# A decoder layer on one core: the first steps written out in another order, a fifth shared group ahead of the sorted experts, and routed rows added by TensorE

## The reference

```python
x = x + attn(layernorm(x))        # 16 heads of 8; att = softmax(q k^T / sqrt(8) * tril(k=-1)); out @ Wr + br
x = x + xattn(layernorm(x), ctx)  # q = x W + b; softmax(q ctx^T) ctx, with 1601 context rows a batch
x = x + ffn(layernorm(x))
# ffn: scores = softmax(x gate^T); the top 2 of 8 experts by scores + bias
#   y = sum over the 2 chosen of weight * (silu(x w1^T) * (x w3^T)) w2^T
#   z = the same MLP with the shared weights sw1, sw2, sw3, for every token
#   result y + z
```

## Time and profile before

| | |
|---|---|
| median of 3 runs | 725.09 us (723.1 to 729.39) |
| the profiled execution | 724.58 us |
| its span, first to last instruction | 722.5 us |
| around the span | 2.08 us |
| TensorE, ScalarE, GpSimd, VectorE busy | 87%, 66%, 64%, 59% of the span |
| mean granted TensorE clock | 0.966 of full speed |

### The profile page before, as it was taken

The page is one execution under the profiler, slowest core; times in us unless marked ns, Lnnn a source line. Parts: engine busy times, 40 slices in busy tenths (PEclk is TensorE's granted clock), DMA queues, the critical chain, the costliest instruction groups (busy, mean ns, idle before and its releaser), DMA issues.

```text
span 722.5 us, 17210 instructions
## 1 busy us (share of the span) xinstructions
PE 631.4 (87%) x5461; PEld 492.1 (68%) x5504; DVE 426.9 (59%) x1166; ACT 477.1 (66%) x1108; POOL 462.6 (64%) x780
## 2 busy tenths in 40 slices
PE   1546789998999999999999999999988679999994
PEld 0323456776767777677776777767877558888883
DVE  1335556686776877768767686775546523333337
ACT  3124558778787787877878778677777326666650
POOL 5034656578787787877877778667654606666660
PEclk9968989999999999999999999999999979999997
DMA  2444354633535235353353433513311223333129
GB/s 71 99 81 133 94 148 132 173 86 108 149 83 157 72 122 149 85 154 97 105 147 82 154 99 102 155 26 109 103 50 60 77 63 99 87 90 89 56 64 308
DMA packets 65110, 77.94 MB, mean 108 GB/s; under 512 B 9314, under 2 KB 50679, under 8 KB 64896
## 3 DMA queue, kind: packets, MB, share of 16 engines
q1 hardware_dynamic: 60672, 68.39, 34.5%
q0 software_dynamic: 4352, 8.47, 3.8%
HBM read 54.30 MB, written 22.64 MB: 106 GB/s over the span
## 4 chain that ended last, share of the span: by engine, by line
PE 37%; POOL 28%; issue 17%; DMA 6%; DVE 4%; SPq 4%; ACT 3%; POOLq 0%; another core or an unknown queue 0%; ACTq 0%; DVEq 0%
PE banks L322 7%; POOL prob L1893 6%; POOL sorted_rows L1918 5%; PE banks L344 4%; PE banks L1010 4%; POOL rstd L1804 3%; PE banks L972 3%; PE banks L752 3%; POOL info_lo L1882 3%; DMA k_stack<-parts 2%; PE banks L333 2%; PE banks L992 2%; POOL qk_r L1831 2%; DMA qst<-q_parts 2%; POOL parts L1833 2%
## 5 line engine op out<-in xcount | busy, mean ns | idle before, releaser
L1332 ACT ACTIVATE prob<-banks 128x512 f32<-128x512 f32 x192 | 114.7, 598 | 67.1 <-PE banks L755 66.5
L1893 POOL TENSOR_SCALAR_AFFINE_SELECT prob<-prob 128x256 f32<-128x256 f32 (+1 forms) x192 | 91.8, 500 | 69.2 <-ACT prob L1332 68.8
L752 PE MATMUL banks<-kst,qst 48*128 48x128 bf16 (+1 forms) x512 | 77.0, 252 | 43.3 <-DMA qst<-q_parts 16.3
L1520 DVE TENSOR_REDUCE mx<-banks 128x2 f32<-128x512 f32 x128 | 86.9, 680 | 33.8 <-PE banks L762 32.8
L1010 PE MATMUL banks<-info,xprobT 128*128 128x128 f32 (+1 forms) x832 | 103.9, 276 | 0.0
L1010 PEld LDWEIGHTS banks<-info,xprobT 128*128 128x128 f32 (+1 forms) x832 | 100.4, 192 | 1.4
L1516 DVE TENSOR_REDUCE mx<-banks 128x4 f32<-128x512 f32 x64 | 44.1, 689 | 73.9 <-remote 39.4
L752 PEld LDWEIGHTS banks<-kst,qst 48*128 48x128 bf16 x512 | 29.2, 95 | 81.2 <-DMA qst<-q_parts 25.2
L1918 POOL DMA_INDIRECT sorted_rows<-row,place x64 | 64.8, 1013 | 24.4 <-issue 18.3
L1551 DVE TENSOR_REDUCE xmax<-banks 128x1 f32<-128x896 f32 x64 | 63.0, 984 | 23.7 <-PE banks L972 18.5
L755 PE MATMUL banks<-qst,kst 51*128 51x128 bf16 (+1 forms) x512 | 75.7, 250 | 0.1
(11 more groups left out here) (193 smaller groups left out, 1591.7 us busy)
## 6 DMA issues: line engine op xcount, KB each, us to landing
infoT<-in_ctxT SPq DMA_DIRECT2D x16, 800.5 KB, 5.3
info<-in_ctx SPq DMA_DIRECT2D x16, 448.0 KB, 3.7
kst<-k_stack SPq DMA_DIRECT2D x32, 192.0 KB
info<-in_ctx SPq DMA_DIRECT2D x16, 320.0 KB
q_parts<-parts SPq DMA_DIRECT2D x32, 96.0 KB, 2.3
k_stack<-parts SPq DMA_DIRECT2D x32, 96.0 KB, 2.3
qst<-q_parts SPq DMA_DIRECT2D x32, 96.0 KB
infoT<-sorted_rows SPq DMA_DIRECT2D x36, 65.0 KB
```

The lines of the kernel that those rows point to most:

```text
L752: pe.matmul(alpha_bank[:, c * w:(c + 1) * w], lhsT=q[:, h, qs], rhs=k[:, h, keys], start=(c == 0), stop=False, skip_group_check=True)
L1332: act.activation(prob[n % 2][:, kind * 512:(kind + 1) * 512], ps[:, gamma_bank_of(b, v), :], ACT.Exp, scale=SCALE).then_inc(s["p_exp"], 1)
L1520: dve.tensor_reduce(mx[:, 1, h:h + 2, 0], bank.rearrange("p (c n) -> p c n", c=2), AX.X, ALU.max).then_inc(s["alpha_max"], 1)
L1893: pool.affine_select(out=w, in_=w, compare_op=ALU.is_gt, fill=0.0, base=0, pattern=[[0, 4 if kind == 2 else 2], [1, P]], channel_multiplie ...
```

## The change

It has four parts.

1. **Head.** The steps -3 to 2 are no longer run by `step(i)`, but written out for each engine in a function `begin()`; the loop starts at 3. The work is the same and the order is another one: both halves of batch 0's parts are written before either is loaded, batch 1 is projected ahead of batch 0's scores, and `x` and the first `infoT` are loaded at the very start. Since the DRAM buffers of the parts are now written sooner, `write_parts` waits until the last `load_stack` of that half has landed.
2. **Banks.** For batches 0 to 2 (`WIDE` = 3), odd units of alpha use bank 0 (6 for batch 0), and for batches 0 and 1 odd units of gamma use bank 1. These banks belong to the cross-attention's scores, which begin after that; its first one waits for alpha and gamma to be done.
3. **Finish.** `EARLY` becomes 5: a fifth shared group runs ahead of the sorted stage. The lists in `finish()` are reordered on every engine but SP.
4. **Tail.** Three shared groups are left. For these TensorE adds the routed rows itself, by multiplying them with the identity matrix into the bank that holds the shared result (`add_routed`, 2 f32 matmuls of 512 columns a group), and VectorE adds that bank to `xall` in one go (`add_late`). Loads and sums run in a mixed order of groups.

The core of the diff, without most of the lists:

```diff
@@ -41,6 +41,7 @@
+WIDE = 3
...
-EARLY = NGR // 2
+EARLY = 5
...
+        LATE_BANKS = (4, 7, 5)
+        SUM_ORDER = (0, 1, 5, 2, 6, 3, 7, 4)
+        BACK_ORDER = (0, 5, 1, 6, 2, 7, 3, 4)
...
-                after(pe, "shared_done", g - 1)
+                    pe.wait_ge(s["shared_done"], EARLY)
                 for t in range(GT):
                     for z in range(2):
-                        mm = pe.matmul(ps[:, Y_BANKS[g % 2], t * D:(t + 1) * D], lhsT=h[g % 2][z][:, t * P:(t + 1) * P],
-                                       rhs=w2_sb[:, E, z, :], start=(z == 0), stop=(z == 1))
+                        mm = pe.matmul(ps[:, LATE_BANKS[g - EARLY], t * D:(t + 1) * D], lhsT=h[g % 2][z][:, t * P:(t + 1) * P],
+                                       rhs=w2_sb[:, E, z, :], start=(t == 0 and z == 0), stop=False, skip_group_check=True)
                 mm.then_inc(s["y_ps"], 1)
+
+            def add_routed(g):
+
+                pe.wait_ge(s[f"back{g}"], 16 * TOPK)
+                for k in range(TOPK):
+                    mm = pe.matmul(ps[:, LATE_BANKS[g - EARLY], :], lhsT=ident, rhs=back[k][:, GT * g:GT * g + GT, :].rearrange("p t d -> p (t d)"),
+                                   start=False, stop=(k == TOPK - 1), skip_group_check=True)
+                mm.then_inc(s["late_ps"], 1)
...
-            def shared(g0, g1):
-                for g in range(g0, g1):
-                    for z in range(2):
-                        shared_up(g, z)
-                    if g > g0:
-                        shared_down(g - 1)
-                shared_down(g1 - 1)
+            def late_groups():
+
+                shared_up(5, 0)
+                shared_up(5, 1)
+                shared_up(6, 0)
+                shared_up(6, 1)
+                shared_down(5)
+                shared_up(7, 0)
+                shared_up(7, 1)
+                shared_down(6)
+                add_routed(5)
+                shared_down(7)
+                add_routed(6)
+                add_routed(7)
...
+            def add_late(g):
+
+                dve.wait_ge(s["late_ps"], g - EARLY + 1)
+                xg = xall[:, GT * g:GT * g + GT, :]
+                dve.tensor_tensor(xg, ps[:, LATE_BANKS[g - EARLY], :].rearrange("p (t d) -> p t d", t=GT), xg, ALU.add).then_inc(s["tokens_done"], 1)
+
             def add_back(g):
                 xg = xall[:, GT * g:GT * g + GT, :]
                 dve.wait_ge(s[f"back{g}"], 16 * TOPK)
                 dve.wait_ge(s["shared_done"], g + 1)
-                for k in range(TOPK):
-                    if k:
-                        dve.wait_ge(s["sum_done"], 2 * g + 1)
-                    dve.tensor_tensor(xg, back[k][:, GT * g:GT * g + GT, :], xg, ALU.add).then_inc(s["sum_done"], 1)
+                final(10 + g, dve.tensor_tensor(xg, back[0][:, GT * g:GT * g + GT, :], xg, ALU.add))
+                dve.tensor_tensor(xg, back[1][:, GT * g:GT * g + GT, :], xg, ALU.add).then_inc(s["tokens_done"], 1)
...
+                for g in SUM_ORDER:
+                    if g < EARLY:
+                        add_back(g)
+                    else:
+                        add_late(g)
...
-        STEPS = range(-3, B)
+        STEPS = range(3, B)
...
-            return G_BANK if b == 0 and u % 2 else A_BANK
+            if u % 2 and b < WIDE:
+                return G_BANK if b == 0 else 0
+            return A_BANK
 
         def gamma_bank_of(b, u):
 
+            if u % 2 and b < WIDE - 1:
+                return 1
             return A_BANK if b == B - 1 and u % 2 else G_BANK
 
...
                 if live(b):
                     sp.wait_ge(s["split_sub"], 2 * b + 2)
+                    after(sp, f"stack{a}_in", 64 * b)
...
+            def begin():
+
+                later_inputs(-1)
+                later_inputs(0)
+                load_infoT(0)
+                write_parts(0, 0)
+                write_parts(0, 1)
+                load_stack(0, 0)
+                load_stack(0, 1)
+                write_parts(1, 0)
+                write_parts(1, 1)
+                load_w13(0)
+                load_stack(1, 0)
+                write_maxima(0)
+                load_info(0, 0)
+                load_stack(1, 1)
+                load_w13(1)
+                later_inputs(2)
...
-            for g in range(NGR):
+            for g in BACK_ORDER:
...
-            for g in range(NGR):
-                sp.wait_ge(s["sum_done"], 2 * g + 2)
+            for n, g in enumerate(SUM_ORDER):
+                sp.wait_ge(s["tokens_done"], n + 1)
...
-                    after(pe, "alpha_max", 12 * b + u - (b == 0))
+                    after(pe, "alpha_max", 12 * b + u - (b < WIDE))
...
-                    after(pe, "p_exp", 12 * old + u - (old == B - 1))
+                    after(pe, "p_exp", 12 * old + u - (old < WIDE - 1 or old == B - 1))
...
+                    if k == 0:
+                        pe.wait_ge(s["alpha_max"], 12 * WIDE)
+                        pe.wait_ge(s["p_exp"], 12 * (WIDE - 1))
...
+            def begin():
+
+                norms_T(-1)
+                query_key(-1)
+                value_heads(0)
+                value_sums(0)
+                norms_T(0)
+                query_key(0)
+                scores(0, 0)
+                scores(0, 1)
+                scores(0, 2)
...
+                early_down(1)
+                early_up(3, 0)
                 norms_T(B + 3)
                 gate_logits(B + 3)
-                early_down(1)
-                early_up(3, 0)
                 early_down(2)
+                early_up(3, 1)
                 ranks(B + 3)
-                early_up(3, 1)
                 early_down(3)
-
+                early_up(4, 0)
+                early_up(4, 1)
+                early_down(4)
...
-                shared_lo(2)
                 deviation3(B - 2)
                 send_rows(B - 3)
+                row_inputs(B - 2)
                 cross_diff(B - 1)
+                shared_lo(2)
                 cross_den(B - 1)
                 cross_weight(B - 1)
-                row_inputs(B - 2)
-                deviation3(B - 1)
                 shared_lo(3)
                 send_rows(B - 2)
+                deviation3(B - 1)
+                shared_lo(4)
                 row_inputs(B - 1)
                 send_rows(B - 1)
-                shared_lo(4)
                 shared_lo(5)
-
+                shared_lo(6)
```

567 lines of the change are left out of this document (433 added, 134 removed).

## The result

In 11 runs of each on one chip, the changed kernel takes 718.99 us (714.86 to 723.03) and the kernel before 727.96 us (722.78 to 735.49). The ratio is 0.989, with a 95% interval of 0.986 to 0.993: about 8 us, or 1.1%, faster. The forecast was 12.6 us. The profiled execution takes 718.32 us with a span of 716.2 us, against 724.58 and 722.5 before: 6.3 us. The sign was right and the size too large, so each term must be held against the trace. In later batches of runs the kernel before took 728.6, 730.5, 754.4 and 761.6 us, and the other kernels moved with it, so each experiment is held against the kernel before of its own batch.

A forecast was written before the change was run, and what follows sets the result against it. TensorE, busy 87% of the span, was read as the main engine, with DMA bounding the tail. The sum was 724.58 - 10.4 (head) + 0.7 (finish) - 0.3 (fifth group) - 2.2 (tail) = 712.4 us profiled; forecast 712.5, range 706 to 719.

The forecast's parts named there:

- The head up to step 2: From the start to maxima_T of step 2: 97.7 to 87.3, a gain of 10.4 us, bounds 4.8 and 16.8.
- order by itself: Head, batch 1: projecting it ahead of the scores starts step 1 at 42.7, 4.8 us earlier.
- The two banks: Head: a unit costs the slower of TensorE (0.7) and VectorE (0.75) instead of 1.56 us; step 2 takes 20.5, not 23.8.
- the banks are not what the units wait for: Rival, head: units wait for the parts, the head gives 4.8 us and the time is 718; chance 0.10.
- the loop's own code is untouched, so I take it as a block that only shifts: Steady loop: stays at 29.8 us a step, with maxima_T of step 15 near 475.5.
- Finish: finish() until the sorted rows are there: 0.4 + 1.6 - 1.3 = +0.7 us, bounds -3 and +4.
- 1.26: finish(): VectorE's 0.57 us wait for sent rows and a 0.69 product ahead of places(15) both go.
- The fifth group: Sorted stage: its ups and down run where TensorE waits for sorted rows; -0.3 us, as the clock may stay up.
- The tail: First routed load to the end: a gain of 2.2 us, between 0 and 4.4, with DMA as the bound.
- the price of the rest: Tail: the 0.81 MB still moved after 718 takes 2.6 us at 316 GB/s, ending at 720.6.
- Its price of an f32 matmul of 512 columns: Tail, TensorE's routed adds: 0.9 us each, between 0.5 and 1.2, 5.4 us in all.
- The gain of 3 us by that page's estimate: Tail: 6.29 MB in 17.6 us at about 358 GB/s, ending near 719.6; the prediction stayed with 316 GB/s.

The follow-up runs named there:

- narrow: The changed kernel with one bank of each kind where it has two for the first batches (WIDE = 1); ratio 1.015 to the kernel before.
- batches 2 and 3: Two later rounds of follow-up runs, each held against its own run of the kernel before, which took 728.6 and 730.5 us.
- four_early: The changed kernel without the fifth early group (EARLY = 4) and with the tail of before; ratio 0.991 to the kernel before.
- after_again: The changed kernel unaltered, run again on another chip; 717.83 us, ratio 0.986 to the kernel before.
- no_head: The changed kernel with the head of before, keeping its new finish(), fifth group and tail; ratio 0.998 to the kernel before.
- mended_slots: The changed kernel with deviation3(15) ahead of send_rows(14), and choices(15), places(15) and slots() ahead of add_shared(2) and hidden(3, 1); 723.62 us, ratio 0.994.
- pool_mended: The changed kernel with only deviation3(15) put back ahead of send_rows(14) on GpSimd; ratio 0.985 to the kernel before.

## Why the forecast was wrong in size, and what of it held

- **The head up to step 2** was forecast at 10.4 us and gave 12.1, in part by luck. The path there was wrong: step 1 was to start at 42.7 and started at 46.23. Batch 0's scores begin 1.7 us later than forecast, its units take 0.9 us each at the low clock, and the maxima are written at 42.88 instead of 39.6. So order by itself gives 1.3 us at step 1, not 4.8, and `narrow` shows that without the banks it costs. The parts of batch 2 still left at 58.10 (forecast 57.5), and from the first unit of step 2 to `maxima_T` it took 18.0 us instead of 20.5. The two banks, which the sum priced at 3.3 us beyond step 2's start, carry some 23 us of this order, together with the clock. The rival "the banks are not what the units wait for" fell. The clock was said to be lowered in three of the four slices behind the third; the row shows two.
- **The step that failed first: "the loop's own code is untouched, so I take it as a block that only shifts"**, with step 3 in it. The faster head asks for batch 3's parts before they are there: step 3's first unit waits for their load, 4.4 us behind `maxima_T` instead of 3.2, and the step is 31.4 us instead of 29.3, and 29.8 to 32.9 in the other profiles with the new head in batches 2 and 3. Some 2 us of the 12.1 go back, of which the wait is 1.2. Up to 1.5 us more went in single longer steps; that those belong to the change isn't shown.
- **Finish** was to cost 0.7 us and costs 3.4 at the first load. `deviation3(15)` begins 75.0 us after `maxima_T` instead of 72.0. Half of that is its place behind the sends, which was priced right at 1.6: put back, it begins 1.5 us earlier. The other 1.5 stay with the fifth group's `early_up` and the other new places, priced at 0.4. The half clock in `early_down(2)` adds 1.4, a term that the sum did not have. From the start of `choices(15)` to the load it is 11.2 us instead of 12.1: the gain of 0.9 for which the sum had 1.26. Together that is 1.5 + 1.5 + 1.4 - 0.9 = 3.5, where 3.4 was measured.
- **The fifth group** under the wait for rows: neutral within 1 us by `four_early`, as forecast. But the ground for the -0.3, that with less idle time the clock may stay up, did not hold: the changed kernel's trace has three stretches at 0.50 between 556.9 and 584.2, as the one before has between 575.0 and 592.1, and two of them now lie ahead of the load.
- **The tail** was forecast at 2.2 us and gives 0.35 (0.7 in `after_again`). The bound was right, the DMA engines, and the step that failed is the price of the rest, 0.81 MB at 316 GB/s in 2.6 us. 17.2 us behind the first routed load the changed kernel has as much left, 2.15 us x 337 + 2.00 us x 68 GB/s = 0.86 MB, and it takes 4.15 us. The engines stay full 2 us longer than before, but then the last stores run out over 2.00 us at 68 GB/s, which the sum had at nothing. Its price of an f32 matmul of 512 columns, 0.9 us for one routed add, was right: a group's two take 1.82 us (701.17 to 702.99).
- The sum used the 316 GB/s of the earlier trace rows. The Trainium skill (DMA: Bandwidth & Descriptors, section Bandwidth) has about 358 GB/s for one core. The runs do not show it as a limit: stretches of 2 us reach 403 GB/s in the kernel before (710.8 to 712.8) and 377 in the changed one (706.85 to 708.85), while the average over 17.2 us stays at 316 to 320. The gain of 3 us by that page's estimate did not come.

By the terms: the sum had 12.2 us (724.58 less 712.4); 1.7 came on top up to step 2, and 2.1 in step 3, 1.5 in the loop, 2.1 between step 15 and the routed loads and 1.9 in the tail went, which leaves 6.3.

## What to carry to other kernels

When a head is made faster, cost the first steady step too: it asks for its inputs earlier, and its DMA round trip may take back what was won. An order with units back to back needs a second bank of every kind that a unit writes; here one kind alone left most of the loss, 102.7 and 107.1 against 109.4 with none and 86 with both. Filler work ahead of a wait is free only as long as nothing on the critical chain stands behind it in a queue, and each such place is read by asking who is behind it; moving a critical item forward can starve the filler and cost more than it wins, all the more where TensorE's clock falls behind the wait. And of a last stretch at low DMA share only a part is work that can be moved forward: the last stores have to run out.

## What the runs showed that was not expected

The clock row does not tell the clock of the head. The windows print a granted clock of 1.00 for `narrow` both in 90 to 108 and in 109 to 140, but the first clock record of its trace is a rise to full at 108.69. The matmuls of `values` take 635 ns ahead of it and 389 ns behind it:

```profile
L851 PE MATMUL banks<-prob,vaug 128*32 128x256 f32 x24 | 3.2, 635 | 0.0
...
L851 PE MATMUL banks<-prob,vaug 128*32 128x256 f32 x40 | 3.2, 389 | 0.0
```

635 ns is what the same form takes where a clock of 0.50 is on record, as in `no_head` from 41.2 to 85.5 (line, then window):

```profile
L813 PE MATMUL banks<-prob,vaug 128*32 128x256 f32 x32 | 4.3, 635 | 0.0
...
41.20:85.50 44.30, 29.09 (x198) 14.93 (x200) 17.42 (x40) 14.62 (x30) 16.39 (x34) 0.50 0.46 113
```

The changed kernel's first record is a rise at 48.27, and its mask matmuls of 256 columns take 396 ns from 28 to 41 and 283 ns from 49 to 68. The kernel before has 396 ns for its own from 26 to 32 and 283 ns from 33 to 39. So these heads ran at half clock at the start, and the changed kernel's batch 0, with units of 0.9 us, lies wholly in it. A forecast of a head should read the clock from the length of one form of matmul, not from the row. That `early_down` takes 3.40 to 3.78 us in some places and 2.03 to 2.05 in others goes with it: in the changed kernel, in `mended_slots` and in `pool_mended` the long ones lie in stretches at 0.50. Why the clock fell in six of ten executions with the same order and the same wait is open.
